# A residual and a bias added on TensorE in PSUM, steps of the attention stage reordered, and its tail rearranged

## What is computed

```python
x = x + tanh(g_xattn[0]) * L0_xattn(layernorm(x), ctx, ctx, mask, ...)   # 16 heads of 8, out: o @ Wo + bo
x = x + tanh(g_ffn[0]) * L0_ffn(layernorm(x), router_w, ...)             # 8 experts, the best 2 of each token
x = x + tanh(g_xattn[1]) * L1_xattn(layernorm(x), ctx, ctx, mask2, ...)  # one head of 128
x = x + tanh(g_ffn[1]) * L1_ffn(layernorm(x), ...)                       # with quantized operands
```

## Time and profile before

| | |
|---|---|
| median of 3 runs | 1026.62 us (1026.48 to 1030.81) |
| profiled execution | 1034.07 us, its span 1032.3 us |
| the stage `layer0` | 0 to 496.9 us of the span, its tail from about 384 us |
| `experts`, `layer1_attention`, `layer1_ffn` | 497 to 755, 755 to 894, 894 to 1032 us |
| mean granted TensorE clock | 0.851 of full speed |
| busy over the span | PE 771.1, DVE 735.3, ACT 634.1, POOL 603.5 us |

### The profile page before, as it was taken

One profiled execution on the slowest core, in us unless ns is written; L12 is line 12 of the kernel. 1 busy time (PEld: TensorE's weight loads), 2 busy tenths in 40 slices (PEclk: granted clock), 3 DMA queues, 4 the chain that ended last, 5 costly groups with the idle time before them and its releaser, 6 DMA issues. The chain is left out here.

```text
span 1032.3 us, 19615 instructions
## 1 busy us (share of the span) xinstructions
PE 771.1 (75%) x6608; PEld 599.7 (58%) x6608; DVE 735.3 (71%) x1656; ACT 634.1 (61%) x1290; POOL 603.5 (58%) x617
## 2 busy tenths in 40 slices
PE   5389998988989888471599999999980688345256
PEld 2367676767767677350477788788760466322145
DVE  4776777788777774123377677778762899869988
ACT  5367676666766645250367677677761587489583
POOL 2155346888887785732046576666774886198500
PEclk9698988899988878785699999999995799767656
DMA  8123311122121114467566677666635833100013
GB/s 224 46 83 76 83 33 68 59 84 99 58 77 56 73 69 141 155 210 142 176 220 216 218 254 247 214 244 242 242 128 173 274 115 114 41 0 1 0 51 113
DMA packets 103826, 132.14 MB, mean 128 GB/s; under 512 B 23840, under 2 KB 78576, under 8 KB 97712
## 3 DMA queue, kind: packets, MB, share of 16 engines
q1 hardware_dynamic: 90240, 110.64, 33.6%
q0 software_dynamic: 9120, 18.91, 5.3%
q10 hardware_dynamic: 4368, 1.34, 0.9%
HBM read 86.59 MB, written 44.18 MB: 127 GB/s over the span
## 5 line engine op out<-in xcount | busy, mean ns | idle before, releaser
L1740 POOL DMA_INDIRECT m_results<-e_y,e_to x156 | 162.7, 1043 | 108.4 <-ACT e_y L1779 67.5
L324 POOL TENSOR_TENSOR a_probs<-a_probs,a_top 128x1024 f32<-128x1024 f32 x64 | 121.8, 1903 | 101.5 <-DVE a_top L958 99.0
L356 POOL DMA_INDIRECT m_tokens_to<-r_rows,r_place x128 | 128.3, 1003 | 46.5 <-issue 33.8
L1755 ACT ACTIVATE e_h<-e_ps_h,e_bias 128x512 f32<-128x512 f32 x156 | 107.0, 700 | 59.4 <-PE e_ps_h L1801 48.7
L1845 DVE TENSOR_TENSOR e_hp<-e_h,e_hp 128x512 fp32r<-128x512 f32 x156 | 110.8, 710 | 5.4
L1843 DVE CAST e_hp<-e_h 128x512 fp32r<-128x512 f32 x156 | 73.4, 471 | 57.7 <-ACT e_h L1755 35.5
L911 DVE TENSOR_TENSOR a_probs<-a_ps_s,a_mask 128x1024 f32<-128x1024 f32 x64 | 78.0, 1219 | 24.9 <-PE a_ps_s L548 24.4
L673 PEld LDWEIGHTS a_ps_o<-a_vals,a_probs_t 128*64 128x64 f32 x2048 | 74.4, 151 | 28.2 <-issue 27.6
L439 ACT ACTIVATE a_gated<-a_ps_o,tanh_gates 128x128 f32<-128x128 f32 x64 | 23.4, 366 | 102.0 <-PE a_ps_o L677 45.1
L673 PE MATMUL a_ps_o<-a_vals,a_probs_t 128*64 128x18 f32 x2048 | 81.3, 222 | 2.7 <-ACT a_heads_t L450 2.2
L694 PE MATMUL a_ps_pt<-ident,a_probs 128*128 128x128 f32 x512 | 80.7, 310 | 0.0
(11 more groups left out here) (291 smaller groups left out, 1984.0 us busy)
## 6 DMA issues: line engine op xcount, KB each, us to landing
e_weights<-m_weights_to SPq DMA_DIRECT2D x39, 1024.0 KB
e_rows<-m_tokens_to SPq DMA_DIRECT2D x39, 264.0 KB
a_ctx_in<-in_ctx_dram SPq DMA_DIRECT2D x32, 256.0 KB
m_weights_to<-r_parts SPq DMA_DIRECT2D x8, 1024.0 KB, 5.0
c_two<-m_results SPq DMA_DIRECT2D x3, 1536.0 KB, 15.9
m_keys_t<-n_keys SPq DMA_DIRECT2D x16, 256.0 KB
m_values<-n_values SPq DMA_DIRECT2D x16, 256.0 KB
c_keys_t<-m_keys_t SPq DMA_DIRECT2D x16, 256.0 KB, 2.7
```

What stands on the lines that cost most here:

```text
L324: pool.tensor_tensor(probs[:, j], probs[:, j], top[:, j].unsqueeze(2).broadcast_to([P, HEADS, SEQ]), ALU.subtract).then_inc(shifted, 1)
L356: pool.indirect_dma_start(tokens_to, bass.IndirectOffsetOnAxis(ap=place[:, k, q:q + 1], axis=0), rows[:, c % RING, q % CT, k, :], None).th ...
L1740: pool.indirect_dma_start(results, bass.IndirectOffsetOnAxis(ap=to[:, v, r:r + 1], axis=0), y[:, v, r], None).then_inc(sent[v], 16)
L1755: act.activation(h[:, c], ps_h[c][:], ACT.Gelu_apprx_tanh, bias=bias[:, n % ROWS, c:c + 1]).then_inc(h_sb, 1)
```

## The change

1. **Residual and bias in PSUM.** Before the product with Wo, PE now adds two matmuls into the same accumulation: the identity times `x_sb` of the tile, and a row of ones (`one`, one partition) times the bias row. POOL scales Wo by the gate once at the start. ACT copies the sum from PSUM straight into `x_sb` (`updated_x`). `gated`, POOL's addition (L339) and DVE's `add_bias` (L893) go. DVE's statistics follow tile by tile.
2. **Order.** PE's `values` move from j = 3 to j = 2 and DVE's from the start of j = 0 to the end of j = 3. PE's context transposes move from before the heads' transpose (L708) to after x's. The router moves from j = 1 to j = 0, the counts from j = 1 of odd steps to j = 2 of even steps, the choices (and ACT's exponential for them) one or two slots earlier, `places` from j = 1 of the odd step to j = 2 of the even one, `gates` two slots earlier, and `low_parts` from j = 3 to j = 1 of the next step.
3. **Scatter.** The lag is 20 slots instead of 23.
4. **Tail.** Keys and values have 8 buffers each (`STAGED`), laid over `spread` and `probs`. The value store moves 2 KB pieces. The 16 slots are 65 to 71 and 75 to 83. The tables are computed in slot 75, in front of slot 76's work on DVE. Each expert's padding is one transfer of whole rows from `pad`, issued by SP between the stores of quads 8 to 15. `pad` grows to 4224 elements per partition; POOL clears it in slot 5 and fills in the row numbers.

```diff
-    NEXT_SLOTS = (65, 66, 67, 69, 70, 71, 74, 75, 76, 78, 79, 80, 81, 82, 83, 84)
-    SCATTER_LAG = 23
+    NEXT_SLOTS = (65, 66, 67, 68, 69, 70, 71) + tuple(range(75, 84))
+    SCATTER_LAG = 20
+    PADS_AT, TABLES_AT = 8, 75
...
     def padding_of(eng, e):
         end = eng.value_load(ends[0:1, e:e + 1], min_val=e * REGION, max_val=e * REGION + NTOK)
-        padding(eng, SPARE + e, end)
+        eng.dma_start(tokens_to[bass.ds(end, RT), :].rearrange("(p r) w -> p r w", p=P), pad[:, e]).then_inc(padded, 16)
...
             if v:
                 store_values(v - 1)
+            e = v - PADS_AT
+            if e == 0:
+                sp.wait_ge(ends_ready, 1)
+            if there(e, EXPERTS):
+                padding_of(sp, e)
...
-                if there(t - 4, TILES) and j % 2:
-                    pool.wait_ge(y_sb, t - 3)
-                    if j == 1:
-                        pool.wait_ge(bo_added, s)
-                    xs = x_sb[:, t - 5:t - 3, :]
-                    pool.tensor_tensor(xs, xs, gated[:, j - 1:j + 1], ALU.add).then_inc(x_out, 1)
...
-        def gate(t, j):
+        def updated_x(t):
             act.wait_ge(o_ps, t - 2)
             act.wait_ge(o_sb, min(t - 2, TILES))
-            if t - 4 >= 4:
-                act.wait_ge(x_out, t // 2 - 3)
-            act.activation(gated[:, j], turn, ACT.Identity, scale=tg[:, 0:1]).then_inc(y_sb, 1)
+            act.activation(x_sb[:, t - 4], turn, ACT.Copy).then_inc(y_sb, 1)
...
                 if there(t - 4, TILES):
-                    mm = pe.matmul(turn, heads_t[:], wo[:], start=True, stop=True)
+                    if t == 4:
+                        pe.wait_ge(bo_set, 3)
+                    pe.matmul(turn, ident[:], x_sb[:, t - 4], start=True, stop=False)
+                    pe.matmul(turn, one[:], bo[0:1], start=False, stop=False)
+                    mm = pe.matmul(turn, heads_t[:], wo[:], start=False, stop=True)
...
-                if j == 1:
-                    c = (s - 5) // 2
-                    if s >= 7:
-                        pe.wait_ge(placed, PLACE_OPS * min((s - 7) // 2, NCH - 1) + 2)
-                    if s % 2 and there(c, NCH):
-                        pe.wait_ge(l_sb, min(s - 3, SUPERS))
-                        counts(c)
-                    if there(s - 3, SUPERS):
-                        router(s - 3)
+                c = (s - 4) // 2
+                if j == 0 and s >= 5:
+                    pe.wait_ge(placed, PLACE_OPS * min((s - 5) // 2, NCH - 1) + 2)
+                if j == 0 and there(s - 3, SUPERS):
+                    router(s - 3)
+                if j == 2 and s % 2 == 0 and there(c, NCH):
+                    pe.wait_ge(l_sb, min(s - 2, SUPERS))
+                    counts(c)
...
-                if there(t - 5, TILES) and j % 2 == 0:
-                    dve.wait_ge(x_out, t // 2 - 2)
-                    for k in range(2):
-                        dve.bn_stats(stats[:, t - 6 + k], x_sb[:, t - 6 + k]).then_inc(stats2, 1)
+                if there(t - 5, TILES):
+                    dve.wait_ge(y_sb, t - 4)
+                    dve.bn_stats(stats[:, t - 5], x_sb[:, t - 5]).then_inc(stats2, 1)
...
                 if j == 3 and there(s + 1, SUPERS):
-                    add_bias(s + 1)
+                    values(s + 1)
...
+                if t == TABLES_AT:
+                    place_tables()
```

More of the change, by code:

```diff
@@ L44 @@
 CTX_RING = 4
+STAGED = 8
 FIRST = 3 * QUAD
@@ L74, in layer0 @@
     heads_t = sb("a_heads_t", [P, P], F32)
-    gated = sb("a_gated", [P, QUAD, DM], F32)
+    one = sb("a_one", [1, P], F32)
     TE = [P, CT, EXPERTS]
@@ L163, in rows_sent, with spare_padding @@
         return 16 * 2 * CT * (c // RING + 1)
-    def padding(eng, n, first):
-        for columns, src in ((slice(0, DM), zeros[:].unsqueeze(1).broadcast_to([P, RT // P, DM])),
-                             (slice(DM, RW), pad[:, n])):
+    def spare_padding(eng, n):
+        first = EXPERTS * REGION + n * RT
+        for columns, src in ((slice(0, DM), pad[:, 0, :, 0:DM]), (slice(DM, RW), spare[:, n])):
             eng.dma_start(tokens_to[bass.ds(first, RT), columns].rearrange("(p r) w -> p r w", p=P), src)\
@@ L494, in _ @@
                 if there(t - 4, TILES):
-                    gate(t, j)
+                    updated_x(t)
                 if there(t - 2, TILES):
                     exponentials(t, j)
-                if j == 0 and there(n, SUPERS):
-                    copy_context(n)
                 if there(t - 3, TILES):
@@ L521, in _ @@
                 c = (s - 4) // 2
-                if j == 3 and s % 2 == 0 and there(c, NCH):
+                if j == 1 and s % 2 == 0 and there(c, NCH):
                     second_weights(c)
@@ L535, in _ @@
         tanh_values(SUPERS - 1)
-        act.wait_ge(ends_ready, 1)
-        for e in range(1, EXPERTS, 2):
-            padding_of(act, e)
     @block.tensor
@@ L697, in _ @@
                         mm.then_inc(pt_ps, 1)
-                if j == 0 and there(n, SUPERS):
-                    transpose_context(n)
                 if j == 1 and there(n, SUPERS):
                     keys(n)
-                if j == 3 and there(n, SUPERS):
-                    values(n)
                 if there(t - 3, TILES):
@@ L720, in _ @@
                     queries(n)
+                    values(n)
                 if j == 3 and there(m, SUPERS):
@@ L903, in _ @@
                 t = s * QUAD + j
-                if j == 0 and there(s, SUPERS):
-                    values(s)
+                if t == 0:
+                    values(0)
                 m = s - 2
@@ L919, in _ @@
                     dve.reciprocal(rsum[:], o[:, :, DH]).then_inc(rsum_ready, 1)
-                c = (s - 5) // 2
-                if j == 1 and there(s - 3, SUPERS):
+                if j == 0 and there(s - 3, SUPERS):
                     take_logits(s - 3)
-                if j == 1 and s % 2 and there(c, NCH):
+                c = (s - 4) // 2
+                if j == 2 and s % 2 == 0 and there(c, NCH):
                     take_counts(c)
```

143 lines of the change are left out of this document (69 added, 74 removed).

## The result

The changed kernel takes 1042.2 us (median of 4 runs, 1039.0 to 1046.7) against 1027.0 us of the kernel before: a ratio of 1.014, 95% interval [1.009, 1.019]. It is slower, by 1.4%. I had forecast 1001 us. The profiled execution takes 1039.73 us (before 1034.07), so the two profiles show 5.7 us of the loss, where the medians show 15.

What follows compares the result with a forecast made beforehand. PE, 90 to 91% busy at a clock near 0.89, was taken to bound the middle part, before a 113 us tail; 1034.07 + 9 (quads) - 34 (tail) = 1009 profiled, 1001 us as median; 8 in 10: 968 to 1027.

Steps and rivals of the forecast that it cites:

- Part 1, the price of the bias product: PE, middle part: two added matmuls cost 0.45 us per tile, 1.8 per quad at full clock; upper bound 0.64 per tile.
- My row for the router: PE: router products with 8 moving columns still take 0.24 us each, so a short side does not make a product cheap.
- The adds taken off GpSimd and VectorE: Attention quads: counted at nothing; at most 1.5 us per quad in the scatter part were PE not the limit.
- Part 2, the period: Middle part: new order saves 0.5 us and costs 0.35; with 1.8 for the products, 20.07 becomes 21.7 us at full clock.
- The clock: PE's mean granted clock, 58 to 376 us: rises from 0.89 to 0.94, so the 15 quads cost +9 us (+28 to -12).
- The rule: Middle part: a quad's period is its period at full clock divided by the mean granted clock; 20.07 / 0.89 gives 22.55.
- The start: Before tile 8: clearing the larger `pad` takes 3.9 us of POOL once; counted 0, at most 4.
- Padding and tables at the end, -17: End of the first stage: padding issued earlier and tables in slot 75 close it 17 to 18 us sooner.
- My walk: Tail, step by step without stalls: last scatters end at 449, the stage closes near 453, 44 us less.
- The stalls, -17 more: Tail: 8 buffers end DVE's waits for stores; tail 23 to 44 us shorter with the padding, 34 taken.
- stalls move: Rival, tail: scatter bursts run the context loads dry, so only the padding's 17 us remain; 1018 us, chance 0.12.
- The slower rival: Rival, PE: added matmuls at half clock; mean clock 0.85 makes quads 25.5 us, +45, in all 1038 us; chance 0.14.

Runs made afterwards that it cites:

- m_fullrow: Changed kernel with the bias product over all 128 rows (1/128 in each) instead of one; ratio 0.987 to the kernel before on the same chip.
- v_fullrow76: Changed kernel with the bias product over 128 rows and the tables in slot 76, behind the gates; ratio 0.999 to the kernel before on the same chip.
- m_rows64: Changed kernel with the bias product over 64 rows (1/64 times the bias) instead of one; one run, 1005.9 us.
- v_best: Changed kernel with 128-row bias product, tables behind the last gates, at most six scatters of a chunk in flight in the tail; ratio 0.987 to the kernel before.
- m_pool_adds: Changed kernel without the two added products: GpSimd adds the residual, VectorE the bias; new order and tail stay; ratio 1.003 to the kernel before.
- m_neither: Changed kernel with residual and bias products both left out, nothing in their place; ratio 0.993 to the kernel before on the same chip.
- t_only: Kernel before with only eight staging buffers, single-transfer paddings between stores and tables in slot 78; old products, order, lag and slots; ratio 0.994.
- c_before2: The kernel before, unchanged, run and profiled again on a chip without the long waits; one run, 999.8 us.
- m_overwrite: Changed kernel with all three products overwriting the bank instead of adding to it, so residual and bias are lost; one run, 1065.9 us.

## Why the prediction was wrong

My sum for the profiled execution was 1009; it took 1039.7. By terms: tile 63 comes 17 us later where I had 9, the tail is 5.7 us shorter where I had 34, and the rest of the span is 5.7 us shorter where I had nothing: 8 + 28 - 6 = 30.

The step that turned the verdict is the price of part 1, and the one that was furthest off is the tail.

- **Part 1, the price of the bias product.** "Three in a row are like the first kind, so two more cost 2 x 0.22 = 0.45 us per tile": that is true of products over 128 rows (m_fullrow: 0.45). The bias product over one row costs 0.61 instead of 0.22, so the pair costs 0.84, above my upper bound of 0.64. My row for the router (8 moving columns) said nothing about fewer rows. The rule that I had cited from the Trainium skill ("TensorE: Matmul & The Clock Gate", LDWEIGHTS) is about the load alone, and there the trace agrees: 0.29 us for the two loads of the bias product, 0.30 for those beside it. In the middle part of the trace of before the only products over fewer rows among full ones are the scores (L548, over 32 rows, 32 in a row), and the prediction doesn't read their edges. The difference is 1.6 us of each quad at full clock, and with it the verdict: full rows take the ratio from 1.024 to 0.999 on chip I (v_fullrow76, tables moved too), and from about 1.009 (m_rows64, one run) to 0.987 on chip III (v_best, tables and bound too).
- **The adds taken off GpSimd and VectorE**, which I counted at nothing. They are worth 1.2 us per quad (m_pool_adds against m_neither). This was in favour of the change, and it is why the pair costs 1.0 us of the quad on balance and not 2.2.
- **Part 2, the period.** Forecast 21.7 us at full clock, with the pair at 0.45. With full rows the pair does cost 0.45, and the quad is 21.43 us at a clock of 0.985, or 21.1 (m_fullrow, chip II), and 22.39 at 0.975, or 21.8 (v_fullrow76, chip I). So that step held but for the price. What I left in the range is there: in the changed kernel the product with the values in slot j = 2 is broken up by gaps of 0.39 and 0.42 us. Whether they are DVE's overrun wasn't tried.
- **The clock.** I took 0.94, and it became 0.98 and 1.00. The direction was right and the size too small; it paid back much of the price.
- **The rule** (quad at full clock / mean clock) gives 23.91 / 0.99 = 24.2 against 23.45 measured. It holds to 3%, since quads differ.
- **The start.** I counted 0, at most 4; it is 3.8. The kernels in the new order have tile 8 at 77.3 to 80.8 us, those in the old one at 74.8 to 76.8, t_only with the large `pad` among them (76.8): it is the order and not `pad`.
- **Padding and tables at the end, -17.** Gone from the end as forecast, and given back. In the two profiles themselves the time from DVE's last value to the close falls from 22.4 us (474.63 to 497.02) to 6.7 (501.70 to 508.42), but the first value comes 6.0 us later after tile 63 (19.6 against 13.6) and the 16 quads take 3.9 us more (81.1 against 77.2): of 15.7 us 5.7 are left. Without the long waits there is a second limit: the scatters end later than the stores, so that padding, tables and buffers moved alone are worth 9 us of tail (t_only). The comparison without long waits shows what the rest of the change does: c_before2 (chip IV) against m_rows64 (chip III, in time the changed kernel). First and last value of DVE and the close, of c_before2:

```profile
395.97 0.69 DVE L974 TENSOR_TENSOR n_values<-a_ps_s,n_bv 128x512 f32<-128x512 f32 x1 [2.79 <-PE a_ps_s L596]
...
442.56 0.69 DVE L974 TENSOR_TENSOR n_values<-a_ps_s,n_bv 128x512 f32<-128x512 f32 x1 [0.83 <-DMA m_values<-n_values]
...
472.11 0.38 SPq L1718 DMA_DIRECT2D e_rows<-m_tokens_to  x1
```

and of m_rows64:

```profile
410.00 0.69 DVE L990 TENSOR_TENSOR a_probs<-a_ps_s,n_bv 128x512 f32<-128x512 f32 x1
...
441.57 0.15 DVE L903 CAST ends<-r_total 1x8 uint32<-1x8 f32 x1
...
450.82 1.28 DVE L990 TENSOR_TENSOR a_probs<-a_ps_s,n_bv 128x512 f32<-128x512 f32 x2
451.77 0.96 POOL L359 DMA_INDIRECT m_tokens_to<-r_rows,r_place  x1 [7.22 <-DVE r_rows L842]
...
465.42 0.69 DVE L990 TENSOR_TENSOR a_probs<-a_ps_s,n_bv 128x512 f32<-128x512 f32 x1 [1.27 <-PE a_ps_s L593]
...
471.93 0.95 POOL L359 DMA_INDIRECT m_tokens_to<-r_rows,r_place  x1 [0.30 <-issue]
482.01 0.37 SPq L1708 DMA_DIRECT2D e_rows<-m_tokens_to  x1
```

  From tile 63 (386.59 and 396.10) the first value comes after 9.4 and 13.9 us, the 16 quads take 46.6 and 55.4, and from the last value to the close it is 29.6 and 16.6. So 13 us won at the end are lost at the start (4.5) and in the quads (8.8). The tables (441.57 to 450) stand between the quads, but in t_only they do too, and its 16 quads take 46.9 us. What t_only hasn't is a second pause of that length: in m_rows64 no quad stands in the slots 72 to 74, and 9.0 us pass between the values of quads 6 and 7 (in t_only, with the old slots, 5.0 at most beside the tables). My walk had the last gates ready 44 us after tile 63, the last scatter at 65 and the close at 69; here they are at 55.7, 75.8 and 85.9. So the walk lost 11 us up to the gates, and it allowed 4 us from the last scatter to the close where it takes 10. Which of order, lag, slots and products cost the tail its 6.5 us on chip II (76.4 in t_only, 82.9 in m_fullrow) was not taken apart further.
- **The stalls, -17 more.** "With 8 buffers no quad waits for a store": true, and DVE's 23.0 us of waits for stores in c_before2 are gone. What they are worth just about covers the tables, which now stand between the quads: in t_only the 16 quads take 46.9 us with both, against 46.6. And the long waits, which I took for late stores, were something else. They stayed: DVE waits 35.0 us for an unrecorded releaser in front of values before, and 23.5 us in front of values and 6.4 in front of the logits after. They stand before instructions with no late DMA in their waits, while POOL has a run of scatters in flight. I had written "that ACT stalls 12.0 us in front of a copy which needs no DMA does not" fit and gone on. The same row speaks against the rule of the Trainium skill that I had weighed ("DMA: Bandwidth & Descriptors", Queues, rings and completion order): late increments of DMAs can't be all of it, as the copy of the logits at 454.15 shows. The rival *stalls move* had the size of the stall term right (nothing gained), but not the place: PE didn't wait for context there.
- **The slower rival**, 0.14, had the right sign and the right engine, but put the loss down to the clock at half, which rose.

## What to carry to other kernels

When pricing an added matmul, compare its number of rows with that of its neighbours. A price read from full products holds only for a full one, so give a bias row the full 128 rows (1/128 in each) when it stands between full products. When a tail has several chains (stores, scatters, tables), ask which one ends it after the change: work taken off the end is won only as far as the next chain. Change slots and lag in a run of their own: here the tail with the old ones was 6.5 us shorter. A wait for an unrecorded releaser in front of an instruction that needs no DMA is a fact to explain before a gain is put on it.

## What the runs showed of the hardware

- A float32 product over 64 rows or over one, between products over 128 rows (all with 128 columns), costs 0.61 us, a full one 0.22 (m_rows64, the changed kernel, m_fullrow), though its load of weights is no longer (0.29 against 0.30 us for the pair of loads in the changed kernel's PEld timeline).
- Whether a product adds to its bank or overwrites it makes no difference here: 0.42 us from start to start both ways (m_overwrite).
- The same kernel takes 1037 to 1040 us on one chip and 995 to 998 on three others. On the slower one DVE and ACT wait up to 16 us in front of work whose matmuls the record shows as done, while GpSimd has a long run of indirect DMAs in flight; with a wait for the landings after every four of them these waits are gone (one profile). By what path the scatters would hold the engines up is open.
